# Attention groups ordered token first, with P transposed in 32x32 blocks by VectorE and V transposed beside the scores

## The chip, the cores and the metric

The kernel runs on all 8 cores of one Trainium2 chip. Each core computes one of the 8 sequences (4096 tokens of width 1024) and the cores don't exchange anything. The metric is the device time in microseconds of the slowest core.

## The reference

One layer: a gated recurrent block with a pre-LayerNorm, then an attention across heads and a dense mixture of 8 experts.

```python
x = x + attn(layernorm(x))            # W_in, silu; W_alpha, W_beta, W_v; scan over tokens; W_out
# ffn, on layernorm(x):
h = rmsnorm(x)
q = (h @ Wq + bq).reshape(b, t, 16, 64)
kv = ((h @ Wdown + bdown) @ Wup + bup).reshape(b, t, 16, 128)
k, v = split(kv, 2, axis=-1)
att = softmax(einsum('bthd,btgd->bthg', q, k) / 8, axis=-1)     # 16 heads x 16 heads, per token
out = einsum('bthg,btgd->bthd', att, v).reshape(b, t, 1024)
x = x + (out @ Wo + bo)
h2 = rmsnorm(x)
gate = softmax(h2 @ Wg + bg)
x = x + einsum('btd,edf,bte->btf', h2, We, gate)                # 8 experts, all of them
```

The attention mixes the 16 heads of one token. No token looks at another.

## The kernel before, in words

Each core walks through 8 tiles of 512 tokens (`NT`, index `t`). A tile passes through these stages in this order: W_in (L391), W_alpha, W_beta and W_v with the scan (L405), W_out (L423), transposes and W_down (L434 to L452), Wq beside Wup (L453, called the projection stage here), attention (L494 to L529), Wo (L535), transposes and the gate (L549 to L567). Every engine has its own program, written out by hand, and semaphores tie them together (names begin with the letter of the engine that raises them: p for TensorE, a for ScalarE, v for VectorE, g for GpSimd).

The experts of tile t-1 are used to fill TensorE's time in the stages of tile t. `ec(t, n)` on TensorE (L341) issues n expert pieces, each of 8 matmuls of 512 columns into bank 6 or 7; `ec(t, n)` on VectorE (L701) adds each piece into the result (L712). A tile has 64 such pieces, of which 34 are spread over the attention (`A_ATT`). Tile 0 has none to spread (`if t == 0: return`), and after the last tile 64 remain.

In the projection stage TensorE makes for each mc of 8 one 8-matmul group of q (two heads) and then two matmuls of Wup (L476, one head of k and v each). ScalarE writes q into `qt` (L652, two per mc) and the v of the even head into `vt` (L659); VectorE writes k into `kt` (L822, two per mc) and the v of the odd head into `vt` (L827). `vt` is R3 seen as bf16, so the trace calls it R. The columns of `qt`, `kt` and `vt` are 64 groups of 128: a group holds 8 tokens and 16 heads, with the head outside and the token inside (column = head slot * 8 + token). A write so puts 8 neighbouring elements (16 bytes) at a time, then jumps on by 256 bytes. Rows 64 to 71 of `qt` and `kt` hold 0/1 and 480 patterns (`qm`, `km`), which add 480 where the token of the query and of the key is the same; the softmax then leaves zero everywhere else.

The attention is done in 16 rounds j of 4 groups. A round j on TensorE is: the scores of j+2 (L489, four matmuls of 128 columns into bank j%2), one expert piece, four transposes of V (L512, 64 rows) and four of P (L515, 128x128) into bank 2+j%2, a second expert piece, and eight small matmuls P.V (L525, 64 columns) into bank 4+j%2. On VectorE it is: the row maximum of j+2 (L833, `smax`), an expert addition, the reciprocal of the row sums of j+1 (L841, `rsum`), one copy of 768 columns of transposed P and V from PSUM to `ptv` (L859), in the first 8 rounds a piece of the next tile's LayerNorm statistics (L723), a second expert addition, and the copy of the P.V result to F1 (L870). ScalarE makes four exponentials per j (L667, with the row sums as a second output) and in rounds 9 and 11 to 14 parts of the next tile's LayerNorm. GpSimd multiplies P by the reciprocals (L291, `pnorm`). P lies in `pb`, three buffers deep; `sml` holds the small vectors.

Of the kernel before, what the change touches and what calls it, by code (L numbers as in the profile page):

```python
# [9 lines left out]
BF16 = mybir.dt.bfloat16  # L10
# [30 lines left out]
def build_program():  # L41
# [43 lines left out]
    ptv = [sb(f"ptv{i}", [128, 768], BF16) for i in range(2)]  # L85
# [52 lines left out]
    p_s, p_ptv, p_o, p_wo = sem("p_s"), sem("p_ptv"), sem("p_o"), sem("p_wo")  # L138
    p_t3, p_gate, p_ec = sem("p_t3"), sem("p_gate"), sem("p_ec")
    a_xp, a_abv, a_sh, a_ln2, a_h = sem("a_xp"), sem("a_abv"), sem("a_sh"), sem("a_ln2"), sem("a_h")  # L140
    a_z, a_q, a_vv, a_p = sem("a_z"), sem("a_q"), sem("a_vv"), sem("a_p")
# [3 lines left out]
    v_mx, v_rs, v_ptv, v_o, v_u = sem("v_mx"), sem("v_rs"), sem("v_ptv"), sem("v_o"), sem("v_u")  # L145
# [192 lines left out]
    def pe_prog(pe):  # L338
# [47 lines left out]
        for t in range(NT + 1):  # L386
# [107 lines left out]
            ec(t, A_S0)  # L494
            score(0)
            ec(t, 1)
            score(1)
            ec(t, 1)
            for j in range(16):
                if j + 2 < 16:  # L500
                    score(j + 2)
                ec(t, 1)
                if j == 0:
                    pe.wait_ge(a_vv, t * 8 + 8)
                    pe.wait_ge(v_vd, t * 8 + 8)
                if j >= 2:
                    pe.wait_ge(v_ptv, t * 16 + j - 1)
                pe.wait_ge(g_pn, t * 16 + j + 1)
                bb = bkb[2 + j % 2]
                for g in range(4):  # L510
                    gg = j * 4 + g
                    pe.transpose(bb[:, 512 + g * 64:512 + (g + 1) * 64],  # L512
                                 vt[0:64, gg * 128:(gg + 1) * 128], idb[0:64, 0:64])
                for g in range(4):
# [14 lines left out]
                mm.then_inc(p_o, 1)  # L529
            ec(t, A_WO)  # L530
# [42 lines left out]
    def act_prog(s):  # L573
# [27 lines left out]
        for t in range(NT):  # L601
# [44 lines left out]
            for mc in range(NCH):  # L646
                s.wait_ge(p_wq, t * 8 + mc + 1)
                qv = qt[0:64, :].rearrange("p (g s) -> p g s", s=128)
                for hl in range(2):
                    h = 2 * mc + hl  # L650
                    off = hl * 64 + mc * 8
                    r = s.activation(out=qv[:, :, off:off + 8],  # L652
                                     in_=bk[mc % 2][64 * hl:64 * hl + 64, :].rearrange("p (g i) -> p g i", i=8),
                                     func=AF.Identity, scale=0.125, bias=cph[:, h:h + 1])
                r.then_inc(a_q, 1)
                hd = 2 * mc
                s.wait_ge(p_wup, t * 16 + hd + 1)
                vv = vt[0:64, :].rearrange("p (g s) -> p g s", s=128)
                s.activation(out=vv[:, :, hd * 8:hd * 8 + 8],  # L659
                             in_=bk[(3, 4, 5, 2)[hd % 4]][64:128, :].rearrange("p (g i) -> p g i", i=8),  # L660
                             func=AF.Identity, bias=cph[:, 32 + hd:33 + hd]).then_inc(a_vv, 1)
# [36 lines left out]
    def dve_prog(v):  # L698
# [66 lines left out]
        for t in range(NT + 1):  # L765
# [229 lines left out]
```

## Time and profile before

| what | value |
|---|---|
| median of three runs | 2069.63 us (2066.82 to 2309.76) |
| the profiled execution | 2072.49 us |
| its span, slowest core (core 2) | 2069.7 us |
| spans of all cores | 2058.9 to 2069.7 us |
| mean granted TensorE clock of the cores | 0.973 to 0.975 |
| busy, TensorE / VectorE / ScalarE / GpSimd | 1954.5 / 1229.8 / 721.7 / 223.2 us |

The profile is one execution on the slowest core. Busy times are sums of instruction durations; neighbouring instructions overlap a little, so what an instruction costs in a full queue is the distance from its start to the next start.

### The profile page before, as it was taken

The page shows a single profiled execution, that of the slowest core. Times are in us where ns is not written, and L with a number is a line of the kernel's source. Part 1 is how long each engine was busy: PE and PEld are TensorE (multiplying, and loading weights), DVE is VectorE, ACT ScalarE, POOL GpSimd, SP SyncE. Part 2 cuts the span into 40 slices and gives each one's busy share as a digit, 9 for nine tenths or more (in the row PEclk, how much of TensorE's full clock was granted, in tenths as well). Part 3 has the DMA queues.
Part 4 walks back from the last instruction along what each step waited for, and adds up shares of the span by engine and source line. Part 5 has one row for each costly group of instructions (what it writes and reads, how often), then busy time and mean ns, then how long its engine had stood idle before and what let it go on. Part 6 is the DMA issues. An engine that isn't in the chain of part 4 may idle for free.

```text
span 2069.7 us, 33009 instructions; the slowest of 8 cores (2058.9 to 2069.7 us)
## 1 busy us (share of the span) xinstructions
PE 1954.5 (94%) x11520; PEld 914.0 (44%) x11520; DVE 1229.8 (59%) x2055; ACT 721.7 (35%) x1905; POOL 223.2 (11%) x225
## 2 busy tenths in 40 slices
PE   4666699999999999999999999999999999999899
PEld 2223344444444444445444444444444444444444
DVE  5447446864577546775468645775467754675544
ACT  2226432533443333542325334433335423342100
POOL 5443100110002100020001100020000200011000
PEclk9876699999999999999999999999999999999999
DMA  8999875665533354334543354333543344433344
GB/s 249 311 315 176 159 196 175 174 173 179 188 113 132 123 204 153 132 123 147 199 143 123 123 185 181 121 125 123 205 162 122 123 153 153 143 102 123 118 147 163
DMA packets 49317, 334.25 MB, mean 161 GB/s; under 512 B 5939, under 2 KB 6067, under 8 KB 14326
## 3 DMA queue, kind: packets, MB, share of 16 engines
q1 hardware_dynamic: 41974, 270.92, 37.6%
q0 software_dynamic: 7184, 61.23, 12.3%
q8 instruction: 97, 1.59, 0.3%
q14 instruction: 62, 0.51, 0.1%
HBM read 317.86 MB, written 48.23 MB: 177 GB/s over the span
## 4 chain that ended last, share of the span: by engine, by line
PE 89%; DMA 5%; DVE 2%; issue 2%; POOL 1%; ACT 1%; DVEq 0%; SPq 0%; ACTq 0%; POOLq 0%
PE bank L359 41%; PE bank L414 14%; PE bank L460 6%; PE bank L542 5%; PE bank L428 5%; PE bank L399 5%; DMA we<-wall 2%; PE bank L489 2%; PE bank L515 2%; PE bank L525 2%; PE bank L476 2%; DMA wscr<-wm 1%; PE bank L512 1%; PE bank L441 1%; PE bank L449 1%
## 5 line engine op out<-in xcount | busy, mean ns | idle before, releaser
L359 PE MATMUL bank<-we,h2T 128*128 128x512 bf16 x4096 | 938.1, 379 | 9.9 <-DVE gat L909 6.5
L712 DVE SCALAR_TENSOR_TENSOR xs<-bank,gat,xs 128x512 f32<-128x512 f32 x512 | 383.9, 750 | 442.3 <-PE bank L359 442.0
L359 PEld LDWEIGHTS bank<-we,h2T 128*128 128x128 bf16 x4096 | 386.8, 98 | 435.8 <-issue 21.0
L414 PE MATMUL bank<-F,wm 128*128 128x512 bf16 x1536 | 339.4, 383 | 20.9 <-POOL wm L278 20.1
L291 POOL TENSOR_TENSOR pb<-pb,sml 128x512 bf16<-128x512 bf16 x128 | 132.9, 1039 | 1440.9 <-DVE sml L841 1440.9
L667 ACT ACTIVATE pb<-bank,sml 128x128 bf16<-128x128 f32 x512 | 181.2, 367 | 217.3 <-DVE sml L833 207.0
L414 PEld LDWEIGHTS bank<-F,wm 128*128 128x128 bf16 x1536 | 151.4, 99 | 207.8 <-issue 31.4
L428 PE MATMUL bank<-wm,F 128*128 128x512 bf16 x512 | 113.7, 384 | 12.0 <-POOL wm L278 12.0
L542 PE MATMUL bank<-wm,F 128*128 128x512 bf16 x512 | 123.2, 384 | 0.7 <-DVE F L870 0.7
L781 DVE SCALAR_TENSOR_TENSOR R<-R 128x512 f32<-128x512 f32 x64 | 49.5, 774 | 122.6 <-ACT R L622 122.6
L460 PE MATMUL bank<-F,wm 128*128 128x512 bf16 x512 | 121.6, 380 | 0.0
L399 PE MATMUL bank<-F,wm 128*128 128x512 bf16 x512 | 112.5, 381 | 0.0
L679 ACT ACTIVATE tm<-R,sml 128x1024 bf16<-128x1024 f32 x32 | 36.7, 1148 | 217.1 <-DVE R L876 217.1
L822 DVE TENSOR_SCALAR kt<-bank,cphs 64x512 bf16<-64x512 f32 x128 | 89.6, 738 | 34.1 <-PE bank L476 33.9
L667 ACT ACTIVATION_READ_ACCUMULATOR pb<-bank,sml 128x1 f32 x512 | 104.7, 204 | 0.0
L652 ACT ACTIVATE qt<-bank,cphs 64x512 bf16<-64x512 f32 x128 | 87.6, 684 | 32.6 <-PE bank L460 31.8
L616 ACT ACTIVATE R<-bank,cpfs 128x512 f32<-128x512 f32 x64 | 44.0, 687 | 155.5 <-DVE F L774 112.6
L876 DVE SCALAR_TENSOR_TENSOR R<-xs,sml,bank 128x512 f32<-128x512 f32 x64 | 47.8, 747 | 80.3 <-PE bank L546 80.3
L833 DVE TENSOR_REDUCE sml<-bank 128x4 f32<-128x512 f32 x128 | 87.2, 682 | 3.1 <-PE bank L489 1.7
L785 DVE TENSOR_TENSOR_SCAN R<-R,hcar 128x512 f32<-128x512 f32 x64 | 83.6, 1307 | 5.2 <-issue 0.4
L428 PEld LDWEIGHTS bank<-wm,F 128*128 128x128 bf16 x512 | 50.5, 99 | 74.1 <-issue 14.9
L542 PEld LDWEIGHTS bank<-wm,F 128*128 128x128 bf16 x512 | 50.3, 98 | 63.1 <-issue 3.8
(93 smaller groups left out, 1645.8 us busy)
## 6 DMA issues: line engine op xcount, KB each, us to landing
we<-wscr SPq DMA_DIRECT2D x128, 1024.0 KB, 4.8
wm<-wscr SPq DMA_DIRECT2D x98, 1024.0 KB, 5.9
wscr<-wall POOLq DMA_DIRECT2D x16, 1024.0 KB, 13.0
out<-xs SPq DMA_DIRECT2D x32, 512.0 KB, 4.3
wscr<-wm POOLq DMA_DIRECT2D x14, 1024.0 KB, 25.5
xs<-x SPq DMA_DIRECT2D x7, 2048.0 KB, 10.8
xs<-wall POOLq DMA_DIRECT2D x12, 1024.0 KB, 23.3
we<-wall POOLq DMA_DIRECT2D x10, 1024.0 KB, 23.1
```

Source lines behind the costliest of these rows:

```text
L291: gp.tensor_tensor(pb[j % 3][:, :].rearrange("p (g n) -> p g n", n=128), pb[j % 3][:, :].rearrange("p (g n) -> p g n", n=128), sml[:, RS + ...
L359: mm = pe.matmul(b[:, :], hT[:, kc * 512 + tb * 128:kc * 512 + (tb + 1) * 128], we[ui % NE][:, kc * 512:(kc + 1) * 512], start=(kc == 0), ...
L399: mm = pe.matmul(bk[4 + mc % 2][:, :], w[:, (mc % 4) * 1024 + kc * 128:(mc % 4) * 1024 + (kc + 1) * 128], F1[:, kc * 512:(kc + 1) * 512], ...
L414: mm = pe.matmul(bk[(mc % 2) * 3 + j][:, :], w[:, (ci % 4) * 1024 + kc * 128:(ci % 4) * 1024 + (kc + 1) * 128], F2[:, kc * 512:(kc + 1) * ...
L428: mm = pe.matmul(bk[u % 4][:, :], F1[:, kc * 512 + tb * 128:kc * 512 + (tb + 1) * 128], (w1 if half else w0)[:, kc * 512:(kc + 1) * 512], ...
L460: mm = pe.matmul(bk[mc % 2][:, :], w[:, (mc % 4) * 1024 + kc * 128:(mc % 4) * 1024 + (kc + 1) * 128], F2[:, kc * 512:(kc + 1) * 512], star ...
L542: pe.matmul(bk[u % 4][:, :], F1[:, kc * 512 + tb * 128:kc * 512 + (tb + 1) * 128], (w1 if half else w0)[:, kc * 512:(kc + 1) * 512], start ...
L652: r = s.activation(out=qv[:, :, off:off + 8], in_=bk[mc % 2][64 * hl:64 * hl + 64, :].rearrange("p (g i) -> p g i", i=8), func=AF.Identity ...
L667: r = s.activation(out=pb[j % 3][:, g * 128:(g + 1) * 128], in_=bk[j % 2][:, g * 128:(g + 1) * 128], func=AF.Exp, bias=sml[:, MX + (j % 3) ...
L712: v.scalar_tensor_tensor(dst, bk[6 + k % 2][:, :], gat[(t - 1) % 2][:, tb * 8 + e:tb * 8 + e + 1], dst, OP.mult, OP.add).then_inc(v_ec, 1)
L822: v.tensor_scalar_add(kv[:, :, hd * 8:hd * 8 + 8], b[0:64, :].rearrange("p (g i) -> p g i", i=8), cph[:, 16 + hd:17 + hd]).then_inc(v_k, 1)
L833: v.tensor_reduce(sml[:, MX + (j % 3) * 4:MX + (j % 3) * 4 + 4], bk[j % 2][:, :].rearrange("p (g n) -> p g n", n=128), axis=AX, op=OP.max, ...
```

## The change

Inside a group the token now stands outside and the head inside (column = token * 16 + head slot, with slot = (head % 2) * 8 + head // 2). The writes of q, k and v therefore put single bf16 elements at a distance of 32 bytes. A 32x32 block on the diagonal of P holds two whole tokens, and everything off these blocks is zero, so transposing each 32x32 block in place gives the transpose of P: VectorE does it from `pb` to `pt` in SBUF, for 512 columns at once, after GpSimd's multiplication. The transposes of P on TensorE and the 768-column copy go. V is transposed on TensorE right behind the scores of the same j, two rounds earlier than before, and ScalarE copies the 256 columns to `vb` ahead of the exponentials of that j. P.V reads `pt` as its moving operand in runs of 8 elements, and the copy to F1 reads PSUM with a distance of 8 fp32 elements between neighbours. The order of VectorE's round is new. The expert pieces are as many as before.

```diff
-    ptv = [sb(f"ptv{i}", [128, 768], BF16) for i in range(2)]
+    pt = [sb(f"pt{i}", [128, 512], BF16) for i in range(2)]
+    vb = [sb(f"vb{i}", [128, 256], BF16) for i in range(3)]
@@ TensorE
+            def vtr(j):
                 if j == 0:
                     pe.wait_ge(a_vv, t * 8 + 8)
                     pe.wait_ge(v_vd, t * 8 + 8)
                 if j >= 2:
-                    pe.wait_ge(v_ptv, t * 16 + j - 1)
-                pe.wait_ge(g_pn, t * 16 + j + 1)
-                bb = bkb[2 + j % 2]
+                    pe.wait_ge(a_vb, t * 16 + j - 1)
                 for g in range(4):
                     gg = j * 4 + g
-                    pe.transpose(bb[:, 512 + g * 64:512 + (g + 1) * 64],
-                                 vt[0:64, gg * 128:(gg + 1) * 128], idb[0:64, 0:64])
-                for g in range(4):
-                    mm = pe.transpose(bb[:, g * 128:(g + 1) * 128],
-                                      pb[j % 3][:, g * 128:(g + 1) * 128], idb[:, :])
-                mm.then_inc(p_ptv, 1)
+                    mm = pe.transpose(bkb[2 + j % 2][:, g * 64:(g + 1) * 64],
+                                      vt[0:64, gg * 128:(gg + 1) * 128], idb[0:64, 0:64])
+                mm.then_inc(p_vt, 1)
+            ec(t, A_S0)
+            for j in range(2):
+                score(j)
+                vtr(j)
                 ec(t, 1)
-                pe.wait_ge(v_ptv, t * 16 + j + 1)
+            for j in range(16):
+                if j + 2 < 16:
+                    score(j + 2)
+                    vtr(j + 2)
+                ec(t, 1)
+                pe.wait_ge(v_pt, t * 16 + j + 1)
+                pe.wait_ge(a_vb, t * 16 + j + 1)
                 if j >= 2:
                     pe.wait_ge(v_o, t * 16 + j - 1)
                 bo = bk[4 + j % 2]
+                pv = pt[j % 2][:, :].rearrange("p (g i l u) -> p g l i u", i=8, l=2, u=8)
                 for g in range(4):
                     for hl in range(2):
                         mm = pe.matmul(bo[64 * hl:64 * hl + 64, g * 64:(g + 1) * 64],
-                                       ptv[j % 2][:, 512 + g * 64:512 + (g + 1) * 64],
-                                       ptv[j % 2][:, g * 128 + hl * 64:g * 128 + (hl + 1) * 64],
+                                       vb[j % 3][:, g * 64:(g + 1) * 64], pv[:, g, hl],
                                        start=True, stop=True)
                 mm.then_inc(p_o, 1)
+                ec(t, 1)
@@ ScalarE
-                qv = qt[0:64, :].rearrange("p (g s) -> p g s", s=128)
+                qv = qt[0:64, :].rearrange("p (n s) -> p n s", s=16)
...
-                    off = hl * 64 + mc * 8
-                    r = s.activation(out=qv[:, :, off:off + 8],
-                                     in_=bk[mc % 2][64 * hl:64 * hl + 64, :].rearrange("p (g i) -> p g i", i=8),
+                    off = hl * 8 + mc
+                    r = s.activation(out=qv[:, :, off], in_=bk[mc % 2][64 * hl:64 * hl + 64, :],
...
             for j in range(16):
+                s.wait_ge(p_vt, t * 16 + j + 1)
+                if j >= 3:
+                    s.wait_ge(p_o, t * 16 + j - 2)
+                s.activation(out=vb[j % 3][:, :], in_=bkb[2 + j % 2][:, 0:256], func=AF.Copy).then_inc(a_vb, 1)
                 s.wait_ge(v_mx, t * 16 + j + 1)
                 if j >= 3:
-                    s.wait_ge(p_ptv, t * 16 + j - 2)
+                    s.wait_ge(v_pt, t * 16 + j - 2)
@@ VectorE
-                kv = kt[0:64, :].rearrange("p (g s) -> p g s", s=128)
-                v.tensor_scalar_add(kv[:, :, hd * 8:hd * 8 + 8],
-                                    b[0:64, :].rearrange("p (g i) -> p g i", i=8),
+                off = (hd % 2) * 8 + hd // 2
+                kv = kt[0:64, :].rearrange("p (n s) -> p n s", s=16)
+                v.tensor_scalar_add(kv[:, :, off], b[0:64, :],
...
             for j in range(16):
+                v.wait_ge(g_pn, t * 16 + j + 1)
+                if j >= 2:
+                    v.wait_ge(p_o, t * 16 + j - 1)
+                v.transpose(pt[j % 2][:, :], pb[j % 3][:, :]).then_inc(v_pt, 1)
                 if j + 2 < 16:
                     smax(j + 2)
-                ec(t, 1)
                 if j + 1 < 16:
                     rsum(j + 1)
-                v.wait_ge(p_ptv, t * 16 + j + 1)
-                if j >= 2:
-                    v.wait_ge(p_o, t * 16 + j - 1)
-                v.tensor_copy(ptv[j % 2][:, :], bkb[2 + j % 2][:, 0:768]).then_inc(v_ptv, 1)
+                ec(t, 1)
...
-                ec(t, 1)
                 v.wait_ge(p_o, t * 16 + j + 1)
                 ov = F1[:, :].rearrange("p (u g i) -> p g u i", u=8, i=8)[:, j * 4:(j + 1) * 4]
-                v.tensor_copy(ov, bk[4 + j % 2][:, 0:256].rearrange("p (g u i) -> p g u i", u=8, i=8)
+                v.tensor_copy(ov, bk[4 + j % 2][:, 0:256].rearrange("p (g i u) -> p g u i", u=8, i=8)
                               ).then_inc(v_o, 1)
+                ec(t, 1)
```

The writes of v into `vt` (both engines) change in the way shown for q and k, and `qm` and `km` get 16 neighbouring columns per token instead of every eighth column.

## Rows read from the trace of the kernel before

**Rows 1.** The page: busy time by engine, and the granted clock in 40 slices.

```profile
PE 1954.5 (94%) x11520; PEld 914.0 (44%) x11520; DVE 1229.8 (59%) x2055; ACT 721.7 (35%) x1905; POOL 223.2 (11%) x225
...
PEclk9876699999999999999999999999999999999999
```

**Rows 2.** The waits of TensorE: total us, times, longest.

```profile
PE bank L525 <- DVE ptv L859: 17.1, 16, 2.3
PE bank L512 <- POOL pb L291: 3.1, 8, 0.9
```

**Rows 3.** Timeline of TensorE, one attention round of tile 4: start, length, instructions.

```profile
1113.48 0.29 PE L512 MATMUL bank<-idbs,R 64*128 64x64 bf16 x4
1113.70 0.40 PE L515 MATMUL bank<-idbs,pb 128*128 128x128 bf16 x4
1113.93 1.89 PE L359 MATMUL bank<-we,h2T 128*128 128x512 bf16 x8
1115.75 0.32 PE L525 MATMUL bank<-ptv 128*64 128x64 bf16 x8
1116.00 0.40 PE L489 MATMUL bank<-kt,qt 72*128 72x128 bf16 x4
1116.23 1.89 PE L359 MATMUL bank<-we,h2T 128*128 128x512 bf16 x8
1118.06 0.29 PE L512 MATMUL bank<-idbs,R 64*128 64x64 bf16 x4
```

**Rows 4.** Timeline of VectorE, the same round.

```profile
1113.65 0.75 DVE L712 SCALAR_TENSOR_TENSOR xs<-bank,gat,xs 128x512 f32<-128x512 f32 x1 [0.62 <-PE bank L359]
1114.32 0.17 DVE L841 RECIPROCAL sml<-sml 128x4 f32<-128x4 f32 x1
1114.41 0.53 DVE L859 COPY ptv<-bank 128x768 bf16<-128x768 bf16 x1
1114.85 0.68 DVE L723 BATCH_NORM_STATS2 bst<-xs 128x6 f32<-128x512 f32 x1
1115.93 0.75 DVE L712 SCALAR_TENSOR_TENSOR xs<-bank,gat,xs 128x512 f32<-128x512 f32 x1 [0.40 <-PE bank L359]
1116.60 0.42 DVE L870 CAST F<-bank 128x256 bf16<-128x256 f32 x1
1116.93 0.68 DVE L833 TENSOR_REDUCE sml<-bank 128x4 f32<-128x512 f32 x1
```

**Rows 5.** Groups by line: busy us, mean ns of one, idle before.

```profile
L667 ACT ACTIVATE pb<-bank,sml 128x128 bf16<-128x128 f32 x512 | 181.2, 367 | 217.3 <-DVE sml L833 207.0 <-PE bank L515 10.3
...
L291 POOL TENSOR_TENSOR pb<-pb,sml 128x512 bf16<-128x512 bf16 x128 | 132.9, 1039 | 1440.9 <-DVE sml L841 1440.9
...
L822 DVE TENSOR_SCALAR kt<-bank,cphs 64x512 bf16<-64x512 f32 x128 | 89.6, 738 | 34.1 <-PE bank L476 33.9
L652 ACT ACTIVATE qt<-bank,cphs 64x512 bf16<-64x512 f32 x128 | 87.6, 684 | 32.6 <-PE bank L460 31.8
L833 DVE TENSOR_REDUCE sml<-bank 128x4 f32<-128x512 f32 x128 | 87.2, 682 | 3.1 <-PE bank L489 1.7
...
L870 DVE CAST F<-bank 128x256 bf16<-128x256 f32 x128 | 53.3, 416 | 6.5 <-PE bank L525 6.3
```

**Rows 6.** Timeline, projection stage of tile 4: its first, a middle and its last writes.

```profile
1084.23 1.40 DVE L822 TENSOR_SCALAR kt<-bank,cphs 64x512 bf16<-64x512 f32 x2 [2.97 <-PE bank L476]
...
1093.70 1.40 DVE L822 TENSOR_SCALAR kt<-bank,cphs 64x512 bf16<-64x512 f32 x2 [0.18 <-PE bank L476]
...
1102.23 0.75 DVE L827 TENSOR_SCALAR R<-bank,cphs 64x512 bf16<-64x512 f32 x1
1102.57 0.39 PE L489 MATMUL bank<-kt,qt 72*128 72x128 bf16 x4
```

**Rows 7.** Timeline of TensorE, attention of tile 0: P.V of two neighbouring rounds.

```profile
187.69 0.42 PE L525 MATMUL bank<-ptv 128*64 128x64 bf16 x8 [0.98 <-DVE ptv L859]
...
190.51 0.42 PE L525 MATMUL bank<-ptv 128*64 128x64 bf16 x8 [0.98 <-DVE ptv L859]
```

More of the change, by code:

```diff
@@ L137, in build_program @@
     p_t2, p_wdn, p_wup, p_wq = sem("p_t2"), sem("p_wdn"), sem("p_wup"), sem("p_wq")
-    p_s, p_ptv, p_o, p_wo = sem("p_s"), sem("p_ptv"), sem("p_o"), sem("p_wo")
+    p_s, p_vt, p_o, p_wo = sem("p_s"), sem("p_vt"), sem("p_o"), sem("p_wo")
     p_t3, p_gate, p_ec = sem("p_t3"), sem("p_gate"), sem("p_ec")
     a_xp, a_abv, a_sh, a_ln2, a_h = sem("a_xp"), sem("a_abv"), sem("a_sh"), sem("a_ln2"), sem("a_h")
-    a_z, a_q, a_vv, a_p = sem("a_z"), sem("a_q"), sem("a_vv"), sem("a_p")
+    a_z, a_q, a_vv, a_p, a_vb = sem("a_z"), sem("a_q"), sem("a_vv"), sem("a_p"), sem("a_vb")
     a_r3, a_h2, a_ge, a_l1, a_l1a = sem("a_r3"), sem("a_h2"), sem("a_ge"), sem("a_l1"), sem("a_l1a")
@@ L144, in build_program @@
     v_st2, v_nm2, v_t2, v_k, v_vd = sem("v_st2"), sem("v_nm2"), sem("v_t2"), sem("v_k"), sem("v_vd")
-    v_mx, v_rs, v_ptv, v_o, v_u = sem("v_mx"), sem("v_rs"), sem("v_ptv"), sem("v_o"), sem("v_u")
+    v_mx, v_rs, v_pt, v_o, v_u = sem("v_mx"), sem("v_rs"), sem("v_pt"), sem("v_o"), sem("v_u")
     v_nb3, v_t3, v_gm, v_gt = sem("v_nb3"), sem("v_t3"), sem("v_gm"), sem("v_gt")
@@ L492, in score @@
                 mm.then_inc(p_s, 1)
-            ec(t, A_S0)
-            score(0)
-            ec(t, 1)
-            score(1)
-            ec(t, 1)
[L499 to L502, printed above, removed]
+            def vtr(j):
                 if j == 0:
@@ L657, in act_prog @@
                 s.wait_ge(p_wup, t * 16 + hd + 1)
-                vv = vt[0:64, :].rearrange("p (g s) -> p g s", s=128)
-                s.activation(out=vv[:, :, hd * 8:hd * 8 + 8],
-                             in_=bk[(3, 4, 5, 2)[hd % 4]][64:128, :].rearrange("p (g i) -> p g i", i=8),
+                vv = vt[0:64, :].rearrange("p (n s) -> p n s", s=16)
+                s.activation(out=vv[:, :, mc], in_=bk[(3, 4, 5, 2)[hd % 4]][64:128, :],
                              func=AF.Identity, bias=cph[:, 32 + hd:33 + hd]).then_inc(a_vv, 1)
             for j in range(16):
+                s.wait_ge(p_vt, t * 16 + j + 1)
+                if j >= 3:
+                    s.wait_ge(p_o, t * 16 + j - 2)
+                s.activation(out=vb[j % 3][:, :], in_=bkb[2 + j % 2][:, 0:256], func=AF.Copy).then_inc(a_vb, 1)
                 s.wait_ge(v_mx, t * 16 + j + 1)
                 if j >= 3:
-                    s.wait_ge(p_ptv, t * 16 + j - 2)
+                    s.wait_ge(v_pt, t * 16 + j - 2)
                 for g in range(4):
@@ L820, in dve_prog @@
                 b = bk[(3, 4, 5, 2)[hd % 4]]
-                kv = kt[0:64, :].rearrange("p (g s) -> p g s", s=128)
-                v.tensor_scalar_add(kv[:, :, hd * 8:hd * 8 + 8],
-                                    b[0:64, :].rearrange("p (g i) -> p g i", i=8),
+                off = (hd % 2) * 8 + hd // 2
+                kv = kt[0:64, :].rearrange("p (n s) -> p n s", s=16)
+                v.tensor_scalar_add(kv[:, :, off], b[0:64, :],
                                     cph[:, 16 + hd:17 + hd]).then_inc(v_k, 1)
                 if hd % 2 == 1:
-                    vv = vt[0:64, :].rearrange("p (g s) -> p g s", s=128)
-                    v.tensor_scalar_add(vv[:, :, hd * 8:hd * 8 + 8],
-                                        b[64:128, :].rearrange("p (g i) -> p g i", i=8),
+                    vv = vt[0:64, :].rearrange("p (n s) -> p n s", s=16)
+                    v.tensor_scalar_add(vv[:, :, off], b[64:128, :],
                                         cph[:, 32 + hd:33 + hd]).then_inc(v_vd, 1)
@@ L850, in dve_prog @@
             for j in range(16):
+                v.wait_ge(g_pn, t * 16 + j + 1)
+                if j >= 2:
+                    v.wait_ge(p_o, t * 16 + j - 1)
+                v.transpose(pt[j % 2][:, :], pb[j % 3][:, :]).then_inc(v_pt, 1)
                 if j + 2 < 16:
                     smax(j + 2)
-                ec(t, 1)
                 if j + 1 < 16:
                     rsum(j + 1)
-                v.wait_ge(p_ptv, t * 16 + j + 1)
-                if j >= 2:
-                    v.wait_ge(p_o, t * 16 + j - 1)
-                v.tensor_copy(ptv[j % 2][:, :], bkb[2 + j % 2][:, 0:768]).then_inc(v_ptv, 1)
+                ec(t, 1)
                 if t + 1 < NT:
@@ L866, in dve_prog @@
                         ln1_nm(t + 1)
-                ec(t, 1)
                 v.wait_ge(p_o, t * 16 + j + 1)
                 ov = F1[:, :].rearrange("p (u g i) -> p g u i", u=8, i=8)[:, j * 4:(j + 1) * 4]
-                v.tensor_copy(ov, bk[4 + j % 2][:, 0:256].rearrange("p (g u i) -> p g u i", u=8, i=8)
+                v.tensor_copy(ov, bk[4 + j % 2][:, 0:256].rearrange("p (g i u) -> p g u i", u=8, i=8)
                               ).then_inc(v_o, 1)
+                ec(t, 1)
             ec(t, A_WO)
@@ L971 @@
     for r in range(8):
-        qm[r, r::8] = 1.0
-        km[r, r::8] = MASKV
+        qm[r, r * 16:(r + 1) * 16] = 1.0
+        km[r, r * 16:(r + 1) * 16] = MASKV
     base = {
```

## The prediction

> **What bounds the kernel now.** I read the page first. TensorE is busy 94% of the span and granted nearly its full clock from the sixth slice of 40 on; no other engine comes above 59% [rows 1]. The list of TensorE's waits says the same: of all waits on the attention's other engines only two are worth a line, 17.1 us for the copied P and V, with 16 waits, and 3.1 us for GpSimd, once per tile [rows 2]. 16 is the number of rounds of one tile, and in tile 0, the only one without expert pieces, each of the two rounds shown waits 0.98 us for the copy [rows 7]. So I take tiles 1 to 7 as bound by what TensorE issues, and tile 0, which has no expert pieces, as bound by a chain through several engines.
>
> The timeline of a round shows this in detail. From one V transpose to the next it is 4.58 us (1113.48 to 1118.06), without a gap on TensorE: 0.22 us for the four V transposes, 0.23 for the four P transposes, 1.82 for an expert piece, 0.25 for P.V, 0.23 for the scores and 1.83 for the second piece [rows 3]. VectorE in the same round is full for 3.56 us and waits twice, 0.40 and 0.62 us, both times for an expert piece [rows 4]; it keeps up and has 1.02 us to spare in the rounds with LayerNorm statistics, and 0.68 us more in the eight without.
>
> **The change part by part.**
>
> *P transposes off TensorE.* Four transposes cost 0.23 us per round, from their start to that of the next piece (1113.70 to 1113.93) [rows 3]. Tiles 1 to 7 have 7 x 16 = 112 rounds, 25.8 us. Bounds: nothing, if another engine takes over the round, and 25.8.
>
> *V transposes moved.* They are as many as before, on the same 64 rows. Now they come behind an expert piece and ahead of the P transposes; then behind the scores and ahead of a piece. Their 0.22 us contain a part that isn't streaming: half as many columns as the P transposes take nearly the same time, and a piece that ends before them or before P.V lasts 1.82 or 1.83 us [rows 3]. Whether changing from the 72-row scores to the 64-row transposes costs more or less than from a piece, no row shows; I take no difference, with 0.1 us a round to either side, 11 us in all, as bounds (about half of the four transposes).
>
> *The first V transpose of a tile* now stands directly behind the first scores and waits for the last v of VectorE. This ends at 1102.98 (1102.23 + 0.75), and the scores start at 1102.57 and take 0.23 [rows 6]: a wait of some 0.2 us. Queued behind it are an expert piece and everything after. Against that stands the wait for GpSimd in the first round, 3.1 us over 8 tiles [rows 2], which moves to P.V(0), one piece later, and should be mostly covered there. I count both together as nothing, and plus or minus 3 us.
>
> *The block transpose on VectorE* replaces the 768-column copy. No row shows one. From below: the copy itself, 0.44 us from its start to the next (1114.41 to 1114.85) [rows 4], and less is possible with only 512 columns. From above I take two passes of the maximum over 512 columns, 2 x 0.68 = 1.36 us. The nearest row is one pass over 512 elements, 0.68 us [rows 5], and I take 0.68. VectorE's round then has 3.56 - 0.44 + 0.68 = 3.80 us in a round of 4.58 - 0.23 = 4.35 us. It costs nothing; TensorE's two expert pieces hide it. It would start to cost at 0.44 + 0.79 = 1.23 us; at the upper bound it is 4.48 us against 4.35 in the 56 rounds with statistics, 7 us.
>
> The Trainium skill, page "VectorE: DVE Perf Modes", section "The three transpose paths", puts a 128x128 bf16 transpose on VectorE at 311 ns. Four times that is 1.24 us as an estimate, which would make the round 4.36 us and leave the sum where it is. No row here shows it.
>
> *VectorE's order.* Its round now begins with a wait for GpSimd, and behind it are queued the maximum of j+2 and the reciprocal of j+1. The reciprocal releases GpSimd about 2 us into the round, the multiplication takes 1.04 us [rows 5], and the next transpose comes only after two expert additions, the statistics and the F1 copy (0.67 + 0.68 + 0.33 + 0.67 = 2.35 us [rows 4]). The wait should therefore be over when VectorE gets there. The transposed P is ready some 1.3 us into the round, P.V needs it after 0.23 + 0.22 + 1.83 = 2.28 us.
>
> *The F1 copy* reads PSUM at a distance of 32 bytes. From below no cost (416 ns now); from above twice the per-element time. One element costs (682 - 416) / 256 = 1.04 ns [rows 5], so 0.27 us more. I take nothing; 3.80 + 0.27 = 4.07 us still fits in 4.35.
>
> *ScalarE's copy of V.* 256 columns; by (684 - 367) / 384 = 0.83 ns per element [rows 5], 0.37 + 0.11 = 0.48 us a round. ScalarE's round has four exponentials, at most 4 x 0.37 = 1.5 us, so it fills 2 of 4.35 us. The copy of j stands ahead of the exponentials of j, but V(j) is transposed right behind the scores, while the maximum still has to be made: hidden.
>
> *P.V with a moving operand in runs of 8 elements.* TensorE streamed 8 x 64 columns in 0.25 us from contiguous memory; no row shows runs. Bounds: nothing, and another 0.25 us a round (28 us). I take nothing, since a run is 16 bytes long and every instruction still reads whole runs.
>
> *The writes of q, k and v* are the uncertain term. They are 24 on VectorE and 24 on ScalarE per tile, as before, but single elements 32 bytes apart. From below no change: today's writes with 16-byte runs take 738 and 684 ns, no more than the 750 ns of contiguous fp32 additions of the same length [rows 4, 5]. From above, twice the per-element time: 512 x 1.04 = 0.53 us more on VectorE, 512 x 0.83 = 0.42 on ScalarE. The cover is thin: VectorE waits just 0.18 us per period of three writes [rows 6], ScalarE 32.6 / 64 = 0.5 us in the mean [rows 5]. I take no change, because both write one element at a time now too, at the engine's own pace; the other end is the first rival.
>
> The Trainium skill, page "SBUF — State Buffer", section "Specifications (TRN2)" (the row on cachelines), says that consecutive accesses at full speed need at least two hits in the same 16-byte line, and that each crossing to another line pays. By that rule the new writes are slowed, with no price given; no row of this trace has such a pattern, so it neither agrees nor disagrees.
>
> *Tile 0.* TensorE has half its clock there (page slices 4 and 5 show a mean of 0.6 [rows 1]) and a round is 2.82 us, with 0.98 us of wait for the copy in it [rows 7]. The P transposes leave that loop. The new loop runs: reciprocal, GpSimd (1.04 us, and 0.25 as my allowance for two handovers), transpose and maximum (0.6 each from start to start, by 0.68 less an overlap of 0.08), reciprocal (0.15): 1.3 + 0.6 + 0.6 + 0.15 = 2.65 us. 16 x 0.17 = 2.7 us less; bounds -8 and +8.
>
> **Sum.** 2072.5 (the profiled execution, its span of 2069.7 and 2.8 around it) - 25.8 - 2.7 = 2044.0 us. The median of the runs shown is 2.9 us below that execution, which gives 2041: I say 2042 us, 1.3% below 2069.6. A measurement of this kernel can tell about 2% from no change.
>
> **Rivals.**
>
> *A: strided writes cost double, and the projection stage becomes bound by VectorE.* Place: L822 and L827. A write now takes 0.71 us from start to start; with 0.53 more it is 1.24. 24 of them from 1084.23 end at 1114.0 instead of 1102.98 [rows 6], 11.0 us later; the scores wait for the last k and the first V transpose for the last v. Eight tiles make 88 us, so 2042 + 88 = 2130 us, slower by 2.9%. It decides from 0.06 us more per write (a third of 0.18), and every further 0.1 us costs 24 x 0.1 x 8 = 19 us. In favour: 2-byte writes each to another place of the memory, and a stage with hardly any slack. Against: no row shows that the distance matters, and the runs of today are free. TensorE would be busy only 64% of that stage, and in tile 0 a TensorE with pauses of 1 us in each round kept only a low clock; this could add to it.
>
> *B: part of this price* (about 0.27 us a write): the last write ends at 1084.23 + 24 x 0.98 = 1107.8, 4.8 us later, 38 us in all: 2080 us.
>
> *C: VectorE bounds the attention.* Transpose at 1.36 us and F1 copy at 0.27 more: 4.75 us against 4.35 in 56 rounds, 22 us given back: 2064 us. For it: the order with waits on GpSimd and TensorE inside; against: more than 0.5 us of slack by my value, and more in the other rounds.
>
> *D: more than I count* (over 41 us off). TensorE would have to lose more than the P transposes; nothing in the rows offers it.
>
> **How the numbers follow.** Forecast 0.49; A 0.28; B 0.12; C 0.08; D 0.03. The forecast's own range is 2030 to 2056 (11 us for the V transposes, 8 for tile 0, 3 for the first round, not all at once). The range must reach to A: 2030 to 2135 leaves out D and the upper part of A. Slower by over 2% (above 2111) is A without its smallest cases, 0.27; faster by over 2% (below 2028) 0.04; within 2% 0.69.
>
> **What would show it.** Right: a round of 4.35 us on TensorE with no waits in it, a VectorE transpose between 0.5 and 0.8 us, L822 and L652 within 20 ns of 738 and 684, the scores of tile 4 some 1.73 us behind the end of the projection stage, and waits of P.V on VectorE only in tile 0. Wrong: L822 or L652 well above, with waits of TensorE for `kt` or R at the start of each attention (A, B); waits of P.V for `pt`, or of expert pieces for VectorE's additions, in rounds 0 to 7 (C); or V transposes that take more than 0.22 us behind the scores.

## The result, and the profile after

The changed kernel takes 2364.78 us (median of 4 runs, 2363.59 to 2366.92) against 2069.07 us; the ratio is 1.1425 with a 95% interval of 1.1382 to 1.1468. It is 14% slower, far outside the range of 2030 to 2135 us. The slowest core's span in the profile is 2365.3 us, and all cores lie between 2354.1 and 2365.3. One of the four runs of the kernel before took 2309.76 us, in the slower state that some executions show, and the ratio is formed without it.

Start with the page of the changed kernel, beside [rows 1].

```profile
PE 2025.8 (86%) x11008; PEld 914.4 (39%) x11008; DVE 1553.8 (66%) x2055; ACT 1091.3 (46%) x2033; POOL 223.7 (9%) x225
...
PE   5664697799977999599996999879997899959999
...
PEclk9775798799978999699997999879997999969999
```

TensorE has 512 instructions fewer, as said, and yet its share has gone from 94 to 86%. VectorE and ScalarE are 324 and 370 us busier, VectorE with the same number of instructions and ScalarE with 128 more (the copies of V, 49.8 us). TensorE's busy share and its granted clock now dip once in each tile, where the clock stood at 9 from the sixth slice on before.

The groups by line say which instructions it is (busy us, mean ns of one, idle before). The line numbers are those of the changed kernel.

```profile
L652 ACT ACTIVATE qt<-bank,cphs 64x512 bf16<-64x512 f32 x128 | 313.1, 2446 | 11.4 <-PE bank L461 9.2
L825 DVE TENSOR_SCALAR kt<-bank,cphs 64x512 bf16<-64x512 f32 x128 | 292.9, 2469 | 25.5 <-PE bank L477 23.7
...
L658 ACT ACTIVATE R<-bank,cphs 64x512 bf16<-64x512 f32 x64 | 170.3, 2660 | 0.0
L829 DVE TENSOR_SCALAR R<-bank,cphs 64x512 bf16<-64x512 f32 x64 | 151.6, 2369 | 2.1
...
L855 DVE STREAM_TRANSPOSE pt<-pb 128x512 bf16<-128x512 bf16 x128 | 90.0, 703 | 19.5 <-POOL pb L292 19.5
...
L490 PE MATMUL bank<-kt,qt 72*128 72x128 bf16 x512 | 55.7, 238 | 67.1 <-ACT qt L652 65.3 <-ACT pb L669 1.8
...
L870 DVE CAST F<-bank 128x256 bf16<-128x256 f32 x128 | 52.3, 408 | 1.6 <-PE bank L525 1.5
...
L664 ACT ACTIVATE vb<-bank 128x256 bf16<-128x256 bf16 x128 | 49.8, 389 | 90.2 <-PE bank L503 89.3 <-issue 0.2
```

The writes of v in the kernel before, which the rows ahead of the prediction don't show:

```profile
L827 DVE TENSOR_SCALAR R<-bank,cphs 64x512 bf16<-64x512 f32 x64 | 48.1, 752 | 2.1
L659 ACT ACTIVATE R<-bank,cphs 64x512 bf16<-64x512 f32 x64 | 43.1, 673 | 0.0
```

A write of 512 single elements takes 2446 ns on ScalarE and 2469 on VectorE, where [rows 5] has 684 and 738. With the writes of v each of the 48 writes per tile is 1.6 to 2.0 us longer, 660 us of busy time in the 384 of a core. No other group of the two engines has moved by anything near that. The block transpose is 703 ns long, the copy to F1 with its strided read of PSUM 408 ns (416 before).

The timeline of TensorE in the projection stage of tile 4 shows what this does to it (the stage that [rows 6] is from).

```profile
1231.30 0.60 PE L477 MATMUL bank<-zb,wupb 64*128 64x512 bf16 x2
1234.13 3.16 PE L461 MATMUL bank<-F,wm 128*128 128x512 bf16 x8 [2.23 <-ACT qt L652]
1237.22 0.97 PE L477 MATMUL bank<-zb,wupb 64*128 64x512 bf16 x2
1241.11 3.31 PE L461 MATMUL bank<-F,wm 128*128 128x512 bf16 x8 [2.92 <-ACT qt L652]
...
1273.02 1.90 PE L360 MATMUL bank<-we,h2T 128*128 128x512 bf16 x8
1283.36 0.58 PE L490 MATMUL bank<-kt,qt 72*128 72x128 bf16 x4 [8.45 <-ACT qt L652]
1285.50 0.37 PE L503 MATMUL bank<-idbs,R 64*128 64x64 bf16 x4 [1.55 <-ACT R L658]
1285.81 3.56 PE L360 MATMUL bank<-we,h2T 128*128 128x512 bf16 x8
```

The period is 6.98 us (1234.13 to 1241.11), three writes of 2.3 us, against 2.37 us before, when TensorE set it. At the end TensorE waits 8.45 us for q and 1.55 for v. By the profile all these waits are for ScalarE, whose last write ends at 1285.26, 0.2 us behind VectorE's. Over the eight tiles its wait for q inside the stage comes to:

```profile
PE bank L461 <- ACT qt L652: 137.6, 48, 4.4
```

The eight matmuls of 512 columns last 3.16 to 3.56 us in most groups, and not 1.9. With pauses of 2 to 3 us between its groups, TensorE is granted the lower of its two clock levels (1.2 and 2.4 GHz) for part of the stage: 0.57 and 0.55 of the full clock in the mean over the groups at 1234.13 and 1241.11, 1.00 over the expert piece at 1273.02, and 0.50 over the one at 1285.81, which follows the waits of 8.45 and 1.55 us. The view by stretches gives the whole stage: 58.40 us, TensorE busy 31.11 of them at a mean clock of 0.77 (behind the length stand the busy time and the instructions of TensorE, its weight load, VectorE, ScalarE and GpSimd, then the clock, the DMA share and GB/s).

```profile
1227.10:1285.50 58.40, 31.11 (x93) 9.47 (x93) 55.55 (x25) 56.56 (x25) 0.00 (x0) 0.77 0.11 36
```

A steady round of the attention does what the prediction said. On TensorE:

```profile
1303.55 0.32 PE L525 MATMUL bank<-pt,vb 128*64 128x64 bf16 x8
1303.80 1.90 PE L360 MATMUL bank<-we,h2T 128*128 128x512 bf16 x8
1305.53 0.39 PE L490 MATMUL bank<-kt,qt 72*128 72x128 bf16 x4
1305.85 0.29 PE L503 MATMUL bank<-idbs,R 64*128 64x64 bf16 x4
1306.07 1.90 PE L360 MATMUL bank<-we,h2T 128*128 128x512 bf16 x8
1307.90 0.32 PE L525 MATMUL bank<-pt,vb 128*64 128x64 bf16 x8
```

From P.V to P.V it is 4.35 us without a gap, against 4.58 in [rows 3].

### The profile page after: what moved, and what is told of

Its sections match the earlier page's. It is cut to its first block, busy times and chain, and to the rows that moved or that the text cites. A ratio compares the mean times of both kernels' runs of the same rounds, so it can differ in the third digit from the quotient of the medians.

```text
span 2365.3 us, 32345 instructions; the slowest of 8 cores (2354.1 to 2365.3 us)
## 1 busy us (share of the span) xinstructions
PE 2025.8 (86%) x11008; PEld 914.4 (39%) x11008; DVE 1553.8 (66%) x2055; ACT 1091.3 (46%) x2033; POOL 223.7 (9%) x225
## 4 chain that ended last, share of the span: by engine, by line
PE 76%; ACT 11%; DMA 6%; issue 3%; DVE 2%; POOL 1%; DVEq 0%; SPq 0%; ACTq 0%; POOLq 0%
PE bank L360 36%; PE bank L415 12%; PE bank L461 8%; ACT qt L652 7%; PE bank L429 5%; PE bank L542 5%; PE bank L400 4%; DMA we<-wscr 2%; ACT R L658 2%; DMA wscr<-wm 2%; PE bank L477 1%; PE bank L525 1%; DMA we<-wall 1%; ACT pb L669 1%; PE bank L503 1%
## 5 line engine op out<-in xcount | busy, mean ns | idle before, releaser
L360 PE MATMUL bank<-we,h2T 128*128 128x512 bf16 x4096 | 951.2, 384 | 15.2 <-DVE gat L910 6.5
L415 PE MATMUL bank<-F,wm 128*128 128x512 bf16 x1536 | 338.6, 383 | 12.2 <-POOL wm L279 11.3
L652 ACT ACTIVATE qt<-bank,cphs 64x512 bf16<-64x512 f32 x128 | 313.1, 2446 | 11.4 <-PE bank L461 9.2
L825 DVE TENSOR_SCALAR kt<-bank,cphs 64x512 bf16<-64x512 f32 x128 | 292.9, 2469 | 25.5 <-PE bank L477 23.7
L461 PE MATMUL bank<-F,wm 128*128 128x512 bf16 x512 | 189.3, 537 | 137.6 <-ACT qt L652 137.6
L415 PEld LDWEIGHTS bank<-F,wm 128*128 128x128 bf16 x1536 | 151.3, 99 | 198.3 <-issue 21.2
L658 ACT ACTIVATE R<-bank,cphs 64x512 bf16<-64x512 f32 x64 | 170.3, 2660 | 0.0
L461 PEld LDWEIGHTS bank<-F,wm 128*128 128x128 bf16 x512 | 58.7, 124 | 260.4 <-issue 244.4
L829 DVE TENSOR_SCALAR R<-bank,cphs 64x512 bf16<-64x512 f32 x64 | 151.6, 2369 | 2.1
L490 PE MATMUL bank<-kt,qt 72*128 72x128 bf16 x512 | 55.7, 238 | 67.1 <-ACT qt L652 65.3
L400 PE MATMUL bank<-F,wm 128*128 128x512 bf16 x512 | 112.7, 381 | 0.0
L855 DVE STREAM_TRANSPOSE pt<-pb 128x512 bf16<-128x512 bf16 x128 | 90.0, 703 | 19.5 <-POOL pb L292 19.5
```

Source lines behind the costliest of these rows:

```text
L360: mm = pe.matmul(b[:, :], hT[:, kc * 512 + tb * 128:kc * 512 + (tb + 1) * 128], we[ui % NE][:, kc * 512:(kc + 1) * 512], start=(kc == 0), ...
L400: mm = pe.matmul(bk[4 + mc % 2][:, :], w[:, (mc % 4) * 1024 + kc * 128:(mc % 4) * 1024 + (kc + 1) * 128], F1[:, kc * 512:(kc + 1) * 512], ...
L415: mm = pe.matmul(bk[(mc % 2) * 3 + j][:, :], w[:, (ci % 4) * 1024 + kc * 128:(ci % 4) * 1024 + (kc + 1) * 128], F2[:, kc * 512:(kc + 1) * ...
L461: mm = pe.matmul(bk[mc % 2][:, :], w[:, (mc % 4) * 1024 + kc * 128:(mc % 4) * 1024 + (kc + 1) * 128], F2[:, kc * 512:(kc + 1) * 512], star ...
L652: r = s.activation(out=qv[:, :, off], in_=bk[mc % 2][64 * hl:64 * hl + 64, :], func=AF.Identity, scale=0.125, bias=cph[:, h:h + 1])
L658: s.activation(out=vv[:, :, mc], in_=bk[(3, 4, 5, 2)[hd % 4]][64:128, :], func=AF.Identity, bias=cph[:, 32 + hd:33 + hd]).then_inc(a_vv, 1)
```

## The experiments

My theory after the profile: the whole loss is the single-element writes, and the rest of the change is worth what was forecast. The rivals: the two engines slow each other down because they write to the same partitions at once; or the new order of the attention costs something too. The third question was what about the write is dear, since that decides whether the change can be saved.

**old_runs: the writes alone put back.**

```diff
-                kv = kt[0:64, :].rearrange("p (n s) -> p n s", s=16)
-                v.tensor_scalar_add(kv[:, :, off], b[0:64, :],
+                kv = kt[0:64, :].rearrange("p (g s) -> p g s", s=128)
+                v.tensor_scalar_add(kv[:, :, hd * 8:hd * 8 + 8],
+                                    b[0:64, :].rearrange("p (g i) -> p g i", i=8),
...
```

> The changed kernel with only the places of q, k and v put back: runs of 8 elements (16 bytes), so the values that the attention works on are permuted and its result differs; all instructions, sizes and waits are those of the changed kernel. Theory 1 (the whole loss is the single-element writes): L652, L825 and the two writes to R fall back to about 690 and 740 ns, a steady attention round stays at 4.36 us, and the time is 2040 to 2048 us, that is 1% below the kernel before. Rival (part of the loss is the new order of the attention itself, or the strided PSUM read of the copy to F1): the writes fall back, but the time stays above 2060 us, with waits of P.V for pt in tiles 1 to 7.

Measured: 2050.9 us against 2068.37, ratio 0.9917 (0.9893 to 0.9941). The writes are back at 684 and 738 ns. So the loss is the writes. But the time is 3 us above the 2040 to 2048 us that I expected, and the waits of TensorE say where that lies.

```profile
PE bank L525 <- DVE pt L859: 32.4, 24, 2.4
...
PE bank L503 <- DVE R L832: 1.4, 8, 0.2
```

P.V waits 24 times for the transposed P: 16 times in tile 0, once in the first round of each later tile (0.9 us), and one time more (0.46 us, late in tile 5). The timeline of such a first round:

```profile
1087.85 0.37 ACT L671 ACTIVATE pb<-bank,sml 128x128 bf16<-128x128 f32 x1
...
1089.97 0.75 DVE L716 SCALAR_TENSOR_TENSOR xs<-bank,gat,xs 128x512 f32<-128x512 f32 x1 [0.93 <-PE bank L360]
...
1090.64 0.17 DVE L846 RECIPROCAL sml<-sml 128x4 f32<-128x4 f32 x1
...
1090.95 1.04 POOL L292 TENSOR_TENSOR pb<-pb,sml 128x512 bf16<-128x512 bf16 x1 [174.94 <-DVE sml L846]
1092.09 0.71 DVE L859 STREAM_TRANSPOSE pt<-pb 128x512 bf16<-128x512 bf16 x1 [1.29 <-POOL pb L292]
...
1093.06 0.32 PE L525 MATMUL bank<-pt,vb 128*64 128x64 bf16 x8 [0.91 <-DVE pt L859]
```

The exponentials end at 1088.2; the reciprocal stands behind an expert addition that waits for TensorE until 1089.97. GpSimd, transpose and P.V come late in a chain, 0.91 us.

**dve_single and act_single: one engine at a time.** In dve_single only k and the odd v are written element by element, in act_single only q and the even v; the others are as in old_runs.

> The changed kernel in which only VectorE writes single elements 32 bytes apart (k and the odd v); ScalarE writes q and the even v in runs of 8 again, so the values are permuted. Theory 1 (each write pays by itself): L825 stays at about 2.4 us, and the time stays near 2340 us, because VectorE alone has 24 x 2.3 = 55 us per tile. Rival 2 (the two engines slow each other down, since they write to the same partitions at the same time): L825 falls to 1.3 us or less, and the time to below 2150 us.

> The mirror image: only ScalarE writes single elements 32 bytes apart (q and the even v), VectorE writes runs of 8; values permuted. Theory 1: L652 stays at about 2.4 us, near 2340 to 2365 us in all, as ScalarE has 24 x 2.35 us per tile too. Rival 2: L652 falls to 1.2 us or less, and the time to below 2150 us.

act_single took 2360.84 us, with L652 at 2400 ns and VectorE's writes at 738. In the first execution of dve_single core 7 had a mean granted clock of 0.178, and six of the eight cores took 4172 to 10135 us, so its time says nothing, and why it happened no run shows; the two cores of ordinary length had L827 at 2431 and 2432 ns. It was run again.

> dve_single once more, because that execution ran at 0.16 to 0.18 of TensorE's clock on core 7 and took up to 10135 us on other cores, while cores 4 and 5 took 2348 and 2356 us with L827 at 2432 ns. Theory 1: an undisturbed execution takes about 2350 us on all cores. Rival: the stretched cores come back, and belong to the kernel.

This time it took 2358.1 us, and all cores 2345.5 to 2356.4. The groups of that execution:

```profile
L827 DVE TENSOR_SCALAR kt<-bank,cphs 64x512 bf16<-64x512 f32 x128 | 288.6, 2431 | 25.5 <-PE bank L477 23.7
...
L652 ACT ACTIVATE qt<-bank,cphs 64x512 bf16<-64x512 f32 x128 | 87.6, 684 | 212.1 <-PE bank L461 211.3
```

Either engine alone pays 2.40 us (ScalarE's q) or 2.43 (VectorE's k) per write; together they pay 2.45 and 2.47. The rival of mutual hindrance falls: it is worth 2% of a write. And mending one engine alone is worth almost nothing (one execution each: 2360.84 and 2358.1 us in place of 2364.78), because the other holds the stage just as long.

**probe_dve, probe_dve2 and probe_act: what makes a write dear.** One extra write ahead of each write of k (or q), with a pattern for each head:

```diff
+                po = [u16[:, 0:512], u16[:, 0:1024:2], ..., u32[:, 0:4096:8]][hd]
+                v.drain()
+                v.tensor_scalar_add(po, pi, cph[:, 16 + hd:17 + hd])
                 kv = kt[0:64, :].rearrange("p (g s) -> p g s", s=128)
```

> old_runs with 16 extra VectorE writes per tile, one ahead of each write of k, each with a drain in front: 512 elements from the same PSUM bank to partitions 64 to 127 of R3, which nobody reads; the pattern changes with the head: bf16 at a distance of 2, 4, 8, 16, 24 and 32 bytes; bf16 in pairs per 16, 32 and 64 bytes; in runs of 4 per 128 bytes and of 8 per 256 bytes; in runs of 8 per 256 bytes with the tokens' loop turned round; fp32 at a distance of 4, 8, 16 and 32 bytes. Theory 1a (a write pays for each new 16-byte line): 740 ns up to a distance of 8 bytes, rising to about 2.4 us from 16 bytes on for bf16 and fp32 alike, pairs about half of the surcharge, runs of 4 a quarter. Rival 1b (it is the 2-byte element written alone, whatever the distance): every pattern of single bf16 elements at 4 bytes and more costs about 2.4 us, fp32 never does. Rival 1c (it is the distance of 32 bytes that hits one bank again and again): 16 and 24 bytes are cheap, 32 is dear in both types.

> old_runs with 16 extra ScalarE writes per tile, one ahead of each write of q, with the same 16 patterns as probe_dve in the same order. Theory (the memory sets the price, not the engine): single bf16 at 16, 24 and 32 bytes near 2.4 us as on VectorE, at 8 bytes about 1.3, fp32 at 16 and 32 bytes about 1.1, everything else 684 ns; since ScalarE makes an element in 0.83 ns and not in 1.04, pairs may stand out by 0.1 us or so. Rival (each engine has its own port with its own price): other ratios than on VectorE.

> probe_dve with 16 other patterns: single bf16 at 6, 10, 12, 14 and 18 bytes; pairs that start at an odd element, per 32 and per 64 bytes; pairs that straddle a 16-byte line, per 64 bytes; runs of 3 per 64 bytes; runs of 4 from an odd element, per 128 bytes; fp32 at 12, 20 and 24 bytes; pairs of fp32 per 32 bytes; 256 single bf16 and 256 single fp32, both at 32 bytes. probe_dve gave 745 ns for pairs, 1.34 us for singles at 8 bytes, 2.35 to 2.47 from 16 on. Theory W (the price is for a 4-byte word written in part): pairs from an odd element touch two words in part each and cost about 2.4 us like singles, whether or not they straddle a line. Theory L (the price is for a new 16-byte line, and what falls into the line that is open is free): odd pairs inside a line cost 745 ns, only the straddling ones are dear; singles rise smoothly from 1.34 at 8 bytes to 2.4 at 16 with the share of writes that open a line (10 bytes: 5 of 8, 14 bytes: 7 of 8). Both: 256 elements cost half of the surcharge.

Some of the rows of probe_dve: bf16 at 4, 8, 16 and 32 bytes, pairs per 16 bytes, pairs per 64 bytes, fp32 at 8 and 16 bytes.

```profile
1154.99 0.78 DVE L855 TENSOR_SCALAR R<-bank,cphs 64x512 bf16<-64x512 f32 x1
1157.40 1.34 DVE L855 TENSOR_SCALAR R<-bank,cphs 64x512 bf16<-64x512 f32 x1
1159.60 2.47 DVE L855 TENSOR_SCALAR R<-bank,cphs 64x512 bf16<-64x512 f32 x1
...
1167.02 2.35 DVE L855 TENSOR_SCALAR R<-bank,cphs 64x512 bf16<-64x512 f32 x1
1171.00 0.75 DVE L855 TENSOR_SCALAR R<-bank,cphs 64x512 bf16<-64x512 f32 x1
...
1174.98 0.74 DVE L855 TENSOR_SCALAR R<-bank,cphs 64x512 bf16<-64x512 f32 x1
...
1184.53 0.74 DVE L855 TENSOR_SCALAR R<-bank,cphs 64x512 f32<-64x512 f32 x1
1186.91 1.11 DVE L855 TENSOR_SCALAR R<-bank,cphs 64x512 f32<-64x512 f32 x1
```

And of probe_dve2: pairs from an odd element per 32 bytes, the same straddling a 16-byte line, and 256 single bf16.

```profile
1185.29 1.28 DVE L856 TENSOR_SCALAR R<-bank,cphs 64x512 bf16<-64x512 f32 x1
...
1190.38 2.35 DVE L856 TENSOR_SCALAR R<-bank,cphs 64x512 bf16<-64x512 f32 x1
...
1207.46 1.28 DVE L856 TENSOR_SCALAR R<-bank,cphs 64x256 bf16<-64x256 f32 x1
```

All of VectorE's, in us for 64 partitions and 512 elements, with the number of 16-byte lines that a write enters:

| pattern | lines entered | measured |
|---|---|---|
| bf16, contiguous | 64 | 0.74 |
| bf16 at 4 / 6 / 8 bytes | 128 / 192 / 256 | 0.78 / 1.06 / 1.34 |
| bf16 at 10 / 12 / 14 bytes | 320 / 384 / 448 | 1.64 / 1.92 / 2.19 |
| bf16 at 16 / 18 / 24 / 32 bytes | 512 | 2.47 / 2.46 / 2.46 / 2.35 |
| 256 bf16 at 32 bytes | 256 | 1.28 |
| pairs on a 4-byte boundary, per 16 / 32 / 64 bytes | 256 | 0.75 / 0.74 / 0.74 |
| pairs from an odd element, per 32 / 64 bytes | 256 | 1.28 / 1.33 |
| pairs that straddle a line, per 64 bytes | 512 | 2.35 |
| runs of 3 per 64 bytes | 170 | 0.95 |
| runs of 4 from an odd element, per 128 bytes | 128 | 0.78 |
| fp32 at 8 / 12 / 16 / 20 bytes | 256 / 384 / 512 / 512 | 0.74 / 0.89 / 1.11 / 1.12 |
| 256 fp32 at 32 bytes | 256 | 0.67 |

One sum fits them to 0.05 us (the patterns at 32 and 64 bytes are up to 0.11 us cheaper than it says): 0.21 us, plus the larger of 1.04 ns per element and a price per line entered. That price is 4.4 ns where a 4-byte word is written in part (from 1.34 at 256 lines and 2.47 at 512: 1.13 us / 256), and 1.8 ns where only whole words are written (1.11 at 512 lines of fp32: 0.90 us / 512). For example the runs of 3: 170 x 4.4 = 0.75, and 0.21 make 0.96; the aligned pairs: 256 x 1.8 = 0.46, less than the 0.53 us of their elements, so they cost nothing extra.

Of what I expected of probe_dve, theory 1a had the place of the rise right but not its start (1.34 us already at 8 bytes), took fp32 to be as dear as bf16, and gave pairs half of the surcharge, where aligned ones pay none. Rival 1b falls: single bf16 cost 0.78 us at 4 bytes, and fp32 pays too, 1.11 at 16. Theory W, that only the word counts, falls: odd pairs inside one line cost 1.28 us, straddling ones 2.35. Theory L by itself falls too: aligned and odd pairs enter equally many lines and cost 0.74 and 1.28. Both hold together. Rival 1c, one bank hit again and again at 32 bytes, falls, as 16, 18 and 24 bytes cost the same or a little more. The sum is fitted to the durations; why the price is what it is, no run shows.

ScalarE's probe has the same shape: 0.83, 1.39, 2.52, 2.50 and 2.39 us at 4, 8, 16, 24 and 32 bytes, fp32 at 16 bytes 1.16, aligned pairs 0.71 per 16 bytes and 0.68 per 64. From 8 to 16 bytes its write grows by 1.13 us as on VectorE, again 4.4 ns per line; with 0.26 us in place of 0.21 and 0.83 ns per element the same sum holds. So the price goes with the pattern that is written, and not with one engine.

**pairs: the change with a cheap write.** A 32x32 block must hold two whole tokens, but their order inside it is free. With the two tokens side by side in each head slot, every write is a pair on a 4-byte boundary, every 64 bytes. The mask rows, the pattern of P.V and the copy to F1 follow.

```diff
-                kv = kt[0:64, :].rearrange("p (n s) -> p n s", s=16)
-                v.tensor_scalar_add(kv[:, :, off], b[0:64, :],
+                kv = kt[0:64, :].rearrange("p (m s i) -> p m s i", s=16, i=2)
+                v.tensor_scalar_add(kv[:, :, off], b[0:64, :].rearrange("p (m i) -> p m i", i=2),
...
-                pv = pt[j % 2][:, :].rearrange("p (g i l u) -> p g l i u", i=8, l=2, u=8)
+                pv = pt[j % 2][:, :].rearrange("p (g m l w) -> p g l m w", m=4, l=2, w=16)
...
-        qm[r, r * 16:(r + 1) * 16] = 1.0
+        c = (r // 2) * 32 + r % 2
+        qm[r, c:c + 32:2] = 1.0
```

> The changed kernel with another order inside the 32-blocks: block = two tokens, column = pair of tokens * 32 + head slot * 2 + token of the pair. A 32x32 block on the diagonal still holds two whole tokens, so VectorE's block transpose still gives the transpose of P, but q, k and v are now written as two neighbouring bf16 (4 bytes) every 64 bytes; qm, km, the moving pattern of P.V and the copy to F1 follow. Theory (what costs is a 2-byte element alone in its word; probe_dve had pairs at 16, 32 and 64 bytes at 745 ns): L652 and L825 fall to at most 760 and 740 ns, and the time is that of old_runs, 2045 to 2055 us, with the reference's result. Rival (in the real stage, with both engines writing and rows read back by TensorE, pairs cost something too): L825 or L652 above 900 ns and a time above 2075 us.

Measured: 2051.25 us, ratio 0.9909 (0.9893 to 0.9924), and its groups:

```profile
L827 DVE TENSOR_SCALAR kt<-bank,cphs 64x512 bf16<-64x512 f32 x128 | 89.7, 739 | 33.8 <-PE bank L477 33.7
L652 ACT ACTIVATE qt<-bank,cphs 64x512 bf16<-64x512 f32 x128 | 89.1, 696 | 32.4 <-PE bank L461 31.6
```

**pairs_early: the first reciprocal of a tile moved up.**

```diff
             smax(1)
-            ec(t, 1)
             rsum(0)
+            ec(t, 1)
```

> pairs with one more edit: VectorE's first reciprocal of a tile stands before the second expert addition, not behind it. In old_runs P.V of round 0 waited 0.91 us in each of tiles 1 to 7, because the reciprocal (1090.64) stood behind an expert addition that waited for TensorE until 1089.97, while the exponentials had ended at 1088.2. Theory: that wait goes, 7 x 0.9 = 6 us less than pairs (2040 to 2048 us). Rival: the exponentials or GpSimd are late next and the gain is under 2 us.

Measured: 2044.47 us, ratio 0.9873 (0.9852 to 0.9894), 6.8 us below pairs as expected. TensorE's waits for the transposed P are one per round of tile 0 and the one in tile 5 (24 in all before); the seven of the first rounds are gone.

```profile
PE bank L525 <- DVE pt L857: 26.0, 17, 2.4
```

This version leaves nothing of the layer out. It is 1.3% faster than the kernel before (under 2%, but the interval is clear of 1) and 13.5% below the changed one.

## Why the prediction was wrong

The step that failed is "The writes of q, k and v", where I took no change. The words of the prediction: "both write one element at a time now too, at the engine's own pace". The runs showed a pace that depends on where the elements go (0.74 us for 512 on VectorE in runs or aligned pairs, 2.35 as singles 32 bytes apart), and the 16-byte runs of the rows hide that. Measured on VectorE, a write costs 1.6 us more from start to start (24 of them from 1229.43 to 1285.04, 2.32 us each, against 0.71). It is the term that the sum put at nothing, and it cost some 300 us.

Rival A named the place and the mechanism, though it had VectorE alone in view where ScalarE's writes take as long and end last. But its upper bound was mis-sized: 0.53 us for "twice the per-element time", where 1.61 was measured. The bound was a choice, not a row: no row had such a pattern, and I let the range end there. In the terms of A the sum comes out: 24 x 1.61 = 38.6 us per tile, less what VectorE had been waiting. The stage of tile 4 measures 58.40 us in the changed kernel and 21.23 in pairs_early (1063.04 to 1084.27), 37.2 us more; the eight stages together take 470.9 us against 169.8, 301 us more. I had noted that a starved TensorE might lose clock, without a price. Inside the stage it didn't matter, since the writes set the pace; behind it, the first expert piece takes 3.38 us in place of 1.72, 11 us in seven tiles. The two make 312 of the 313.5 us between pairs and the changed kernel.

The rule of the Trainium skill that I had weighed, page "SBUF — State Buffer", section "Specifications (TRN2)", says that full speed needs two or more hits in a 16-byte line. For whole words the trace agrees (fp32 at 8 bytes 0.74 us, at 16 bytes 1.11); for single bf16 it is milder than what was measured, 0.78 us already at 4 bytes and 1.34 at 8. Rival A stood for this rule with a chance of 0.28 and a range that ended at its bound; by what was measured both were too small.

The other steps, against old_runs, pairs and pairs_early:

- P transposes: right. The round went from 4.58 to 4.35 us, by 0.23.
- V transposes behind the scores: nothing in sum, as forecast, but because two changes cancel, and that was luck. The scores now take 0.32 us in place of 0.23, the piece ahead of them 1.73 in place of 1.83; the V transposes still take 0.22.
- The block transpose: I took 0.68 us, it is 703 ns long and 0.63 from start to start. The estimate of 1.24 us, four times the 311 ns that the Trainium skill gives on its page "VectorE: DVE Perf Modes", section "The three transpose paths", was too long by half a microsecond. The transpose hides behind the expert pieces, and rival C falls: P.V waits behind it in one steady round of tiles 1 to 7, for 0.46 us.
- The copy to F1 with 32 bytes between its reads of PSUM: nothing (408 ns). P.V with runs of 8: nothing (0.25 us). ScalarE's copy of V: 0.39 us, I had 0.48; hidden.
- The first round of a tile: mis-sized. I counted the later wait of P.V(0) as "mostly covered"; it was 0.91 us, and the first V transpose added the forecast 0.2 (1.4 us in 8 tiles). Moving one reciprocal gave 6.8 us back. The forecast had the wait for GpSimd in view, not that the reciprocal ahead of it was queued behind an expert addition.
- Tile 0: 2.73 us per round in old_runs (182.57 to 185.29 is 2.72), I had 2.65 against 2.82 before. From its first to its last P.V it is 42.38 us against 43.70, half of the 2.7 us forecast.

With free writes the change takes 2051.25 us (pairs), 9 us above the forecast of 2042 and inside its own range of 2030 to 2056. The 2044.47 us of pairs_early need the moved reciprocal, which the forecast didn't contain.

## What to carry to other kernels

When a new layout turns a contiguous or 16-byte write into single 2-byte elements, price the write itself and not only its count: 512 bf16 elements in lines of their own took 2.4 us and not 0.7, on VectorE and ScalarE alike. Look for a layout with two neighbouring elements on a 4-byte boundary: here it served as well and cost nothing, since the block transpose only asked that both tokens of a block stay in it. And where no row of the trace has the pattern, an upper bound of twice is a wish: ask what stage would be bound by it, and leave the range open on that side.

## What the runs showed of the hardware that I had not expected

The price of a scattered write to SBUF comes in two sizes, by the sum fitted to the probes: 4.4 ns per 16-byte line entered where a 4-byte word is written in part, and 1.8 ns where words are whole. Alignment alone decides between 0.74 and 1.28 us for the same number of pairs. Reads of PSUM at 32 bytes cost nothing on VectorE (408 ns against 416 for 256 fp32 elements). And both engines can pay the write price at the same time with hardly any mutual hindrance (2.40 and 2.43 us alone, 2.45 and 2.47 together).
